# Front and tail of a convolution, quantised dense and residual kernel written out by hand, with kernel blocks loaded singly, tile 0 seeded by VectorE and tile 30 finished by VectorE

## What is computed

```python
c   = conv1d(x, weight, kernel 9, pad 4, groups 4)        # float32
c   = c + (cond @ c_weight.T)[:, :, None] + fside_S_0[None, :, None]
xq  = fq(c, bits=8, axis=-1)                              # per row of 1024 positions
kq  = fq(ffn_kernel, bits=8, axis=0)                      # 1024 x 1024, per column
y   = einsum('bsd,df->bsf', xq, kq) + fq(bias, bits=16)
out = x + fq(y, bits=8, axis=-1)
```

## Time and profile before

| | |
|---|---|
| median of 3 runs | 258.36 us (258.27 to 258.91) |
| the profiled execution | 258.86 us, with a span of 256.8 us in the trace |
| outside the span | 2.06 us |
| TensorE busy | 234.9 us (91%) |
| VectorE, ScalarE, GpSimd busy | 204.6, 187.2, 189.0 us |
| moved by DMA | 56.03 MB |

### The profile page before, as it was taken

How to read it: one execution, slowest core, us unless ns; L and a number is a source line. 1 busy time by engine, 2 the same in 40 slices (tenths; PEclk the granted TensorE clock), 3 DMA queues, 4 the chain that set the end, 5 groups by cost and what they waited for, 6 DMA issues and landing times.

```text
span 256.8 us, 3977 instructions
## 1 busy us (share of the span) xinstructions
PE 234.9 (91%) x1298; PEld 149.8 (58%) x1320; DVE 204.6 (80%) x418; ACT 187.2 (73%) x187; POOL 189.0 (74%) x135
## 2 busy tenths in 40 slices
PE   7697989999999999999999999999999999998900
PEld 3366666666666666666656666665666666663400
DVE  1488999366788888778997897899789889869782
ACT  6588679874677777858678759867876995955661
POOL 5473333079999888897849995995998599566990
PEclk9999999999999999999999999999999999999975
DMA  6999230122227697889789899799999999899667
GB/s 227 404 411 375 91 144 11 75 84 85 82 29 225 111 351 190 175 242 235 181 180 301 233 243 284 187 259 346 211 245 287 264 223 285 209 292 335 122 202 290
DMA packets 15652, 56.03 MB, mean 218 GB/s; under 512 B 1680, under 2 KB 1808, under 8 KB 15632
## 3 DMA queue, kind: packets, MB, share of 16 engines
q1 hardware_dynamic: 11312, 40.77, 43.2%
q0 software_dynamic: 4032, 14.68, 32.9%
q10 hardware_dynamic: 288, 0.33, 0.4%
HBM read 39.00 MB, written 16.78 MB: 217 GB/s over the span
## 4 chain that ended last, share of the span: by engine, by line
POOL 45%; issue 41%; DMA 5%; DVE 4%; SPq 1%; ACT 0%; PE 0%; DVEq 0%; POOLq 0%
POOL y L280 21%; POOL x_lo L272 15%; POOL y L302 7%; DMA k_raw<-ffn_kernel 3%; DMA x_sb<-x_rows 2%; DVE k_max L670 2%; POOL y L292 1%; POOL y L306 1%; POOL y L295 1%; DVE a_int L746 0%; DVE y_max L768 0%; ACT k_int L376 0%; SPq L233 0%; SPq L210 0%; DVE x_sb L777 0%
## 5 line engine op out<-in xcount | busy, mean ns | idle before, releaser
L566 PE MATMUL dense_ps<-kq,a_t 128*128 128x512 bf16 x475 | 113.8, 379 | 1.4 <-ACT kq L385 0.3
L272 POOL TENSOR_TENSOR x_lo<-xwin,x_hi 128x1032 fp32r<-128x1032 f32 x32 | 80.3, 2511 | 45.6 <-ACT x_hi L362 45.6
L280 POOL TENSOR_TENSOR y<-y,bq 128x512 f32<-128x512 f32 x59 | 77.1, 1384 | 4.9 <-DVE y L703 4.9
L566 PEld LDWEIGHTS dense_ps<-kq,a_t 128*128 128x128 bf16 x496 | 47.5, 101 | 45.8 <-issue 0.5
L717 DVE TENSOR_REDUCE small_ps<-conv_ps 128x8 f32<-128x1024 f32 x32 | 39.3, 1228 | 21.3 <-PE conv_ps L517 21.2
L416 ACT ACTIVATE y_int<-y,y_inv 128x1024 int16<-128x1024 f32 x31 | 35.6, 1149 | 25.5 <-DVE y_inv L758 25.5
L703 DVE SCALAR_TENSOR_TENSOR y<-dense_ps,row_scale,k_scale_b 128x512 f32<-128x512 f32 x57 | 42.4, 745 | 4.7 <-PE dense_ps L566 4.6
L401 ACT CAST a_t<-turn_ps 128x1024 bf16<-128x1024 int16 x32 | 32.3, 1011 | 17.4 <-PE turn_ps L550 17.4
L517 PE MATMUL conv_ps<-x_hi,w_hi 128*128 128x512 f32 x128 | 40.8, 440 | 1.7 <-ACT x_hi L362 1.7
L746 DVE TENSOR_TENSOR a_int<-conv_ps,inv 128x1024 int16<-128x1024 f32 x32 | 39.2, 1224 | 0.5 <-DVE inv L738 0.5
L768 DVE TENSOR_REDUCE y_max<-y 128x1 f32<-128x1024 f32 x31 | 37.5, 1209 | 2.4 <-POOL y L280 2.4
(11 more groups left out here) (65 smaller groups left out, 152.6 us busy)
## 6 DMA issues: line engine op xcount, KB each, us to landing
xwin<-x_windows SPq DMA_DIRECT2D x32, 516.0 KB, 6.8
out<-y SPq DMA_DIRECT2D x31, 512.0 KB, 4.8
y<-x_rows POOLq DMA_DIRECT2D x28, 512.0 KB, 7.4
k_raw<-ffn_kernel SPq DMA_DIRECT2D x4, 1024.0 KB, 12.3
x_sb<-x_rows SPq DMA_DIRECT2D x4, 512.0 KB, 6.1
w_raw<-taps SPq DMA_DIRECT2D x2, 256.0 KB, 2.9
b_row<-ffn_bias SPq DMA_DIRECT2D x1, 512.0 KB, 11.9
out<-x_sb SPq DMA_DIRECT2D x1, 256.0 KB, 2.5
```

The lines of the kernel that those rows point to most:

```text
L272: pool.tensor_tensor(x_lo[:, at].rearrange("p n b -> p (n b)"), xwin[:, t % XWIN, :], x_hi[:, at].bitcast(F32).rearrange("p n b -> p (n b) ...
L280: pool.tensor_tensor(y[:, t % YRING, half(h)], y[:, t % YRING, half(h)], bq[:, half(h)], ALU.add).then_inc(s["biased1" if h else "biased_e ...
L566: mm = pe.matmul(dense_bank(t, h), a_t[:, t % LEVELS, q].rearrange("b j o -> b (j o)"), kq[:, q, half(h)], start=(q == 0), stop=(q == Q - 1))
```

## The change

Every engine's loop now runs from k = 8 to 24; what comes ahead of it and behind it is written out call by call, in a new order, on all engines.

- The kernel blocks are loaded one by one (8 DMAs of 512 KB in place of 4 of 1 MB) and their maxima are taken one by one (`k_maximum`, `k_scales`).
- The spread of the context weights (`spread_c`) and the seed of tile 0 go from ScalarE to VectorE; `WARM`, `WARM_G0`, `WARM_X` go from 5, 2, 5 to 3, 1, 2.
- `by_dma(t)` now holds for t < 30: tiles 28 and 29 get x by the accumulating DMA too. `EARLY` and the special cases go; the bias of tile 28's first half is added by GpSimd.
- Tile 30 is rounded by ScalarE (`round_y`) and finished by VectorE in one instruction (`finish`): `y_int` times scale plus x into `x_sb`, which is stored from there.
- The order of the tail's stores on SyncE's queue is new.

```diff
-WARM, WARM_G0, WARM_X, EARLY = 5, 2, 5, 4
+WARM, WARM_G0, WARM_X = 3, 1, 2
 LAST = TILES - 1
-ACT_T = LAST - 2
+WAYS = {LAST - 2: "AA", LAST: "VV"}
+HEAD = 8
+TAIL = LAST - 6
...
         def by_dma(t):
-            return t < LAST - 3
+            return t < LAST - 1
...
+            def load_k(fb):
+                sp.dma_start(k_raw[:, fb, :], ker[fb]).then_inc(k_in[fb], 16)
...
             def store(t):
+                if t == LAST - 1:
+                    sp.wait_ge(s["finished"], 1)
+                    sp.dma_start(out[t], x_sb[:, nth_pool(t) % XRING, :]
+                                 ).then_inc(stored[t % YRING], 16)
+                    return
...
+            load_xwin(LAST - 3)
+            load_x(LAST - 1)
+            load_xwin(LAST - 2)
+            store(LAST - 12)
+            load_xwin(LAST - 1)
+            load_xwin(LAST)
+            store(LAST - 8)
+            store(LAST - 13)
+            store(LAST - 11)
+            store(LAST - 10)
+            store(LAST - 6)
+            store(LAST - 9)
+            store(LAST - 4)
+            store(LAST - 5)
+            store(LAST - 7)
+            load_x(LAST)
+            store(LAST - 3)
+            store(LAST - 2)
+            store(LAST - 1)
             store_last(sp, 0)
...
+            split(LAST - 1)
+            add_bias(LAST - 6, 1)
+            add_bias(LAST - 5, 1)
+            add_x(LAST - 8)
+            split(LAST)
+            add_bias(LAST - 5, 0)
+            add_x(LAST - 7)
+            add_bias(LAST - 4, 1)
+            add_bias(LAST - 4, 0)
+            add_x(LAST - 6)
+            add_bias(LAST - 3, 0)
+            add_x(LAST - 5)
+            add_bias(LAST - 3, 1)
+            add_x(LAST - 4)
+            scale_and_add(LAST - 2, 0)
+            scale_and_add(LAST - 2, 1)
+            add_bias(LAST - 1, 0)
+            add_x(LAST - 3)
+            add_bias(LAST - 1, 1)
+            add_x(LAST - 2)
...
             conv(0)
             conv_start(1)
-            k_turn(0)
             spread_max(0)
-            k_turn(1)
+            k_turn(0)
             conv_rest(1)
             turn_levels(0)
+            k_turn(1)
+            spread_max(1)
             conv(2)
             k_turn(2)
-            spread_max(1)
-            k_turns(3, 4)
             turn_levels(1)
-            dense(0, 0)
+            k_turn(3)
             conv_start(3)
+            k_turn(4)
             spread_max(2)
             conv_rest(3)
+            dense(0, 0)
             turn_levels(2)
+            conv_start(4)
             dense(1, 0)
...
+            conv(LAST)
+            dense(LAST - 2, 0)
+            turn_levels(LAST - 1)
+            spread_max(LAST)
+            dense(LAST - 2, 1)
             dense(LAST - 1, 0)
             turn_levels(LAST)
             dense(LAST - 1, 1)
...
+                if g == 0:
+                    dve.wait_ge(s["ctx_made"], 1)
+                    dve.tensor_copy(conv_cols(0), ctx_cols[:, 0, 0:NS].unsqueeze(2)
+                                    .to_broadcast([P, NS, BLOCKS])).then_inc(s["seeded_first"], 1)
...
+            def finish(t):
+                at, i = t % 2, nth_pool(t)
+                dve.wait_ge(x_in[i % XRING], nth(i, XRING))
+                dve.wait_ge(s["y_rounded"], t + 1)
+                dve.scalar_tensor_tensor(out=x_sb[:, i % XRING, :], in0=y_int[:, at],
+                                         scalar=y_scale[:, at:at + 1], in1=x_sb[:, i % XRING, :],
+                                         op0=ALU.mult, op1=ALU.add).then_inc(s["finished"], 1)
```

More of the change, by code:

```diff
@@ L147, in outs, with way, done, acts @@
             return [t for t in range(LAST) if second_step(t) + (2 if t < NEAR else 1) == k]
[L149 to L158, removed]
+        def way(t, h):
+            return WAYS.get(t, "GG")[h]
+        def done(t, h, ways):
+            return sum(way(u, h) in ways for u in range(t + 1))
+        def acts(t, h):
+            return sum(way(u, i) == "A" for u in range(t + 1) for i in range(2) if u < t or i <= h)
         def dense_bank(t, h):
@@ L277, in add_bias @@
             def add_bias(t, h):
-                wait(pool, f"scaled{h}", but_act(t))
+                wait(pool, f"scaled{h}", done(t, h, "VG"))
                 wait(pool, "b_made", 1)
@@ L306, in add_x @@
                 pool.tensor_tensor(to, to, x_sb[:, i % XRING, :], ALU.add).then_inc(s["added"], 1)
[L308 to L312, removed]
+            split_w(0)
+            split_w(1)
+            split(0)
+            split(1)
+            split(2)
+            split(3)
+            split(4)
+            split(5)
+            split(6)
+            split(7)
+            split(8)
+            add_bias(0, 1)
+            add_bias(0, 0)
+            add_bias(1, 0)
+            split(9)
+            add_bias(2, 0)
+            add_bias(3, 0)
+            for k in range(HEAD, TAIL):
                 for t in seconds(k - 1):
@@ L467, in _ @@
[L467 to L481 removed]
+            take_levels(6)
@@ new lines, in _ @@
+            round_x(9)
+            for k in range(HEAD, TAIL):
+                seed(k + 1)
+                take_levels(k - 1)
+                round_x(k + 2)
+                for t in outs(k):
+                    quantise(t)
+            seed(LAST - 5)
+            round_x(LAST - 4)
+            take_levels(LAST - 7)
+            quantise(LAST - 11)
+            round_x(LAST - 3)
+            seed(LAST - 4)
+            take_levels(LAST - 6)
+            quantise(LAST - 10)
+            seed(LAST - 3)
@@ L708, in add_bias @@
             def add_bias(t, h):
-                wait(dve, f"scaled{h}", but_act(t))
+                wait(dve, f"scaled{h}", done(t, h, "VG"))
                 wait(dve, "b_made", 1)
@@ L809, in _ @@
             column_max(4)
-            k_levels(3)
+            k_maximum(7)
+            k_scales(3)
             scale_half(2, 0)
             levels(4)
-            for k in range(5, TILES):
+            column_max(5)
+            scale_half(3, 0)
+            levels(5)
+            column_max(6)
+            levels(6)
+            scale_half(4, 0)
+            column_max(7)
+            scale_half(0, 1)
+            bias_scale()
+            scale_half(5, 0)
+            levels(7)
+            scale_half(1, 1)
+            for k in range(HEAD, TAIL):
                 again = seconds(k)
@@ new lines, in _ @@
+            scale_half(LAST - 5, 1)
+            levels(LAST - 3)
+            column_max(LAST - 2)
+            out_scale(LAST - 6)
+            scale_half(LAST - 4, 1)
+            levels(LAST - 2)
+            scale_half(LAST - 4, 0)
+            out_scale(LAST - 5)
+            column_max(LAST - 1)
+            out_scale(LAST - 4)
+            scale_half(LAST - 3, 0)
+            scale_half(LAST - 3, 1)
+            levels(LAST - 1)
+            column_max(LAST)
+            out_scale(LAST - 3)
```

380 lines of the change are left out of this document (241 added, 139 removed).

## The result

The changed kernel took 259.19 us (median of 20 executions, 258.22 to 262.55), the kernel before beside it 258.25 us (20 executions, 257.26 to 259.18). The ratio is 1.0041, with a 95% interval of 1.0021 to 1.006: slower by 0.4%, a small difference that the interval just tells from none. Executions over 1.5% above the fastest of their kernel are left out of the ratios: three here, of 262.11 us and more, and one of 257.23 us in experiment 12. The forecast was 260.0 us; the profiled execution took 258.22 us, the shortest of the 20, with a span of 256.5 us where 258.0 had been forecast.

The account below looks back on a forecast made before the run. TensorE, busy 234.9 of 256.8 us, was taken as the bound, with time to gain only in front and tail; 183.5 to tile 25's convolution plus a DMA-bound 74.5 gave span 258.0, time 260.0 us, range 254.0 to 262.5.

Parts of the forecast that it names:

- The front: Before tile 8's convolution: new order fills TensorE's waits, -3.2 us (bounds 1.7 and 4.5), first convolution staying at 8.84.
- The hole in the tail: SyncE's queue: stores held behind tile 23's from about 199 to 220, until its accumulation lands; then four in a row.
- The stall for store 18: Tail, VectorE: tile 28's first write waits 1.4 to 4 us for store 18, hidden while DMAs set the end.
- The pile: DMA work left after the hole: 6 accumulations at 2.85 and 14 plain transfers at 1.35, 36.0 us.
- The whole tail: From tile 25's convolution to the span's end: DMA-bound, 74.5 us, turning the front's -3.2 into +1.2 overall.
- One of the signs: End of the tail: `finish` and the last VectorE instruction would both wait for x.
- The sum: Whole span: 183.5 + 74.5 = 258.0 against 256.8, +1.2; forecast time 260.0 us.
- Transfers overlap: Rival, tail: vector chain sets the end, span 251.5 to 253, if x 31 lands before u = 63; chance 0.27.
- The front gives nothing: Rival: filled gaps open on another engine, the tail's DMA loss stays, 262 to 263; chance 0.10.
- The clock falls ahead of conv(0): Rival, front: fewer ones idle TensorE, half clock makes 8 of conv(0)'s matmuls 1.7 us slower, 261.7; chance 0.07.
- Level: Rival: both signs cancel, low DMA prices and a front of 3.2 to 4, 256.8 to 258.9; chance 0.18.

Follow-up runs that it names:

- experiment 12: Kernel before with the changed front, old loop and tail, x 31 loaded right behind x 30, and 3, 1, 2 matmuls on ones: 252.98 us, ratio 0.9783.
- experiment 9: Changed front with 5, 2, 5 matmuls on ones, loop and tail from k = 8 as in the kernel before: 254.76 us, ratio 0.9852.
- experiment 1: Changed kernel with the matmuls on ones back at 5, 2, 5: 259.28 us, ratio 1.0028.
- experiment 7: Changed kernel with 5, 2, 5 ones, tiles 28 and 29 back to plain x loads and GpSimd additions: 253.88 us, ratio 0.9828.
- experiment 4: Changed kernel with 5, 2, 5 ones, tail stores in tile order and x 31 loaded ahead of store 20: 254.75 us, ratio 0.986.
- experiment 11: Changed kernel, tail and all, with 3, 1, 0 matmuls on ones in place of 3, 1, 2: 260.08 us, ratio 1.0071.
- experiment 2: Changed kernel with tail stores in tile order and x 31 loaded ahead of store 20, ones kept at 3, 1, 2: 255.03 us, ratio 0.9877.
- experiment 5: Changed kernel with 5, 2, 5 ones and tail stores in tile order, x 31's load left between stores 27 and 28: 255.89 us, ratio 0.9889.
- experiment 6: Changed kernel with 3, 1, 0 ones, tail stores in tile order and x 31 loaded ahead of store 20: 255.95 us, ratio 0.9892.

## Why the prediction was right, and where its numbers were off

**The front** was forecast at -3.2 us. By tile 8's convolution the profile has 62.16 - 58.10 = 4.1: 0.74 because the first convolution started at 8.10 and not at the 8.84 that was taken as fixed (it started between 7.3 and 9.2 in the profiles of these experiments, so this part is chance), and 3.3 in work and waits, 50.0 us against 53.3 before. The forecast had added up 62.35 for the kernel before, 0.2 too late, and 50.3 us for the change. The place of the new waits was right too: conv(2) starts 9.8 us after the first, as forecast. Experiment 9 gives 3.8 us (3.1 to 4.6) at the end of the program. In the profiled execution the front gave about 1 us more than forecast, mostly by its starting point.

**The hole in the tail** was forecast from about 199 to 220: it is from 197 to 218.91. Tile 23's accumulation landed at 218.89, forecast 220.0, and four stores went in a row. From the start of tile 25's convolution (182.50, forecast 183.5) that is 36.4 us against 36.5. The stall for store 18 was 1.82 us (forecast 1.4 to 4).

**The pile** was forecast at 36.0 us of DMA work, with 1 us ahead of it and about 1 for the landing: 38.0 from the landing of tile 23's accumulation to the end of the span (220.0 to 258.0). Measured 256.5 - 218.9 = 37.6. The whole tail was forecast at +4.4 us (the sum's +1.2 and the front's 3.2); experiments 1 and 9 make it 4.5. The price of an accumulation came out at 2.96 us by the q0 row, 3.02 before, and x 31 landed at 250.56 ("after 246"). One of the signs didn't come: VectorE's last instructions waited for x, but `finish(30)` waited for nothing, since its x was loaded at 183. The Trainium skill ("Trainium Kernel Development and Optimization", Key Constraints) has all queues share the 16 DMA engines; experiment 7 agrees: with two transfers of GpSimd's queue taken out of the pile, the kernel ends 5.2 us sooner, and x 31 on SyncE's queue is no longer waited for.

**The sum.** Span 258.0 forecast, 256.5 measured: 1.05 of the difference is the front's landmark (59.15 against 58.10), the rest the tail. The median, 259.19 against 260.0, is nearer, and that is luck: the profiled execution was the shortest of the 20, and nine of them lie above 260, most likely through a rival that the forecast gave 0.07.

**The rivals.** *Transfers overlap*: no; the share is 1.0 to 1.06 at 274 to 301 GB/s from 224 to 248. x 31 landed 68.1 us after tile 25's convolution started, and 63 was to decide. Its end of 251.5 to 253 did come, in experiment 4 (252.7), once the same transfers went out in another order; the forecast took the order of issue as given and did not price it. *The front gives nothing*: no, by experiment 9. *The clock falls ahead of conv(0)*: given 0.07, and too low. Here the forecast treated it as all or nothing, and it is a matter of the single execution. The profiled one had a clock of 1.00 from 2 to 20 us after a wait of 0.98, the upper nine have the half-clock time of experiment 11's fall, experiment 1 has no such group, and experiment 2 shows the fall with the same ones. That these nine had their fall in the front is inferred from that, not seen in a profile of theirs. The price was forecast at 1.7 us; by tile 8 it is 1.0, and the two groups of the changed kernel lie about 2.5 apart. *Level*: its range went to 258.9, and the median came out 0.3 above it.

**What stays open**: what the place of x 31 costs once the stores are in order (experiment 5), why the changed kernel's two groups lie further apart than the 1.0 us that a fall costs by tile 8, whether that fall is all that sets them apart, and where the 33 us at half clock of one execution in experiment 12 were.

## What to carry to other kernels

Read the tail by its issuing queue: one store that waits for late data holds every transfer behind it, and what the DMA engines don't do in that hole they do at the end; here one list of issues was worth 4.3 us, and one load moved up 1.8 us in either kernel. How much a hole costs depends on the work behind it: with two accumulations less there, the kernel with the same hole took 253.88 us in place of 259.28. When an addition is moved from an engine into an accumulating DMA, price it in DMA time (2.96 us for 512 KB against 1.44 for a plain transfer in this kernel), and ask whether the DMA engines or the vector engines are full at that place. A change of several parts can come out level because one part gives what another takes: joining the new front to the old tail gave 3.8 us that the whole change hid.

## What the runs showed of the hardware

Idle stretches of 1.88 us (experiment 6), 2.02 us (experiment 2) and 2.28 us (experiment 11), each behind small and few multiplications, were followed by a granted clock of 0.50 to 0.72 in the windows from 8 to 12 us. Those of 0.98 us (the changed kernel) and 1.09 us (experiment 12), behind the same ones as in experiment 2, were not. So with the same program ahead of it the stretch has a different length from one execution to the next, and 3 of 8 executions of experiment 11 had 18 us or more at half clock. One profile of such a kernel says little of its median.

By the packets' time in the pages, the accumulating DMA takes twice the DMA engines' time of a plain transfer of the same bytes, in every kernel here (2.93 to 3.04 against 1.42 to 1.45 us for 512 KB). A plain load issued behind the pile took 9.70 us to land where the share was 1.03.
